# A new order of the instructions in one beat of a software-pipelined attention loop

## The chip, the core and the metric

The kernel runs on one core of a Trainium2 chip. The core's engines run in parallel, each through its own list of instructions and in that order, and they meet at semaphores: PE (TensorE, matrix products and transposes), DVE (VectorE), ACT (ScalarE), POOL (GpSimd) and SP (SyncE, here only DMA issues). The metric is the device time of one execution in microseconds, the median of several runs.

## The reference, cut to what matters

The program is a chain of four blocks: a gated linear recurrence over x of shape (8, 256, 128), six layers of windowed attention and gated feed-forward, one multi-head attention with low-rank projections, and a mixture of experts. Only the six layers are touched here. One of them, for one batch of 256 tokens:

```
qkv = shift_tokens(x) @ Wqkv            # 16 heads of 64
q, k = l2norm(q) * qs, l2norm(k) * ks
q = q*cos*scale + rotate_half(q)*sin*scale
k = k*cos/scale + rotate_half(k)*sin/scale
attn = softmax(mask(q @ k^T * 8))       # windows of 32, each sees 64 keys
x = x + (attn @ v) @ Wo
xn = layernorm(x) * g + b
a, gate = split(xn @ W1 + b1)
x = x + (a * gelu(gate)) @ W2 + b2
```

With 6 layers and 8 batches this is done 48 times. All of it is in float32.

## The kernel before

The 48 (layer, batch) pairs are the iterations i of one flow. In an iteration the attention is cut into four units (two halves of the heads times two halves of the tokens, each 128 tokens by 512 channels), and time is cut into five beats, j = 0 to 4. A unit goes through five stages, and the stages of different units overlap: in beat j the engines work on up to five units of two iterations at once.

- Stage Q (beats 0 to 3): PE multiplies q into bank 0 (L505), k into bank 1 (L507) and v into bank 2 (L539). ACT squares q (L628) and k (L642) into `sq` and copies v (L647). DVE multiplies q and k by the rotary tables, two instructions each (L723, L724). POOL adds the two products (L813, L816) and folds the squares (`sqh`, L819), and DVE sums them (L751).
- Stage T (beats 4, 0, 1, 2): POOL scales q and k by their inverse norms (L807; DVE computes these in beat 4, L701 to L706), PE turns them, q into bank 3 (L478) and k into bank 4 (L487); ACT copies them to `qT` (L661) and to `kBD` (L674, two instructions).
- Stage S (beats 0 to 3): ACT seeds bank 5 with the mask (L613), PE adds the scores (L565), DVE takes the row maximum `mx` (L746), ACT the exponentials `pr` (L666, eight instructions).
- Stage P (beats 1 to 4): PE turns `pr` into bank 6 (L516), ACT copies it to `pT` (L632), PE multiplies by v (L579), DVE sums `pr` (L731) and divides (L763).
- Stage O (beats 2, 3, 4, 0): PE turns the result into bank 4 (L529, in beat 0 L551), ACT copies it to `attT` (L637); after every second unit PE multiplies by Wo (L598).

Bank 4 is thus used twice in a beat: by the k transposes of stage T, which ACT drains with L674 (semaphore `kt_ev`), and by the transposes of stage O in the next beat, which therefore wait for that L674. Bank 1 serves the next k product once its readers are done: DVE's rotation first, ACT's square after it. `sq` is written by both squares and read by L819.

Beside the units there is the feed-forward part. Layernorm (L339 and L346 in beat 1, L353, `ln_scale` at L399 and `xnF` at L681 in beat 3), the up-projection in beat 4 (`up_pe`, L460, three chunks of which the third uses bank 6), Gelu in beat 4 (L655, with a table load before it, L623, and one after it, L657, since the exponentials need another table) and the down-projection in beat 0 (L468).

Nothing schedules at run time. The order on each engine is the order in which the functions below write it, one function for each engine, with `has(F_x)` telling whether a stage has a unit in this beat. Iterations 0 to 2 and 47 to 50 are written out, with parts missing; 3 to 46 are a loop.

Of the kernel before, what the change touches and what calls it, by code (L numbers as in the profile page):

```python
# [13 lines left out]
ALU = mybir.AluOpType  # L14
ACT = mybir.ActivationFunctionType
# [69 lines left out]
def mixed_kernel(nc, A, out):  # L85
    with ExitStack() as ctx:
# [404 lines left out]
        def layers_pe(pe):  # L491
            pe.matmul(bank[5][:, :], ident, cst("rot"), start=True, stop=True).then_inc(s_set.sem, 1)
            for i, j, live, has, unit in units(pe):
                if has(F_Q):
                    _, _, n = unit(F_Q)
                    h, t = j // NT, j % NT
                    xt = xs[:, t * P:(t + 1) * P]
                    if j == 0:
                        pe.wait_ge(xs_in.sem, xs_in.after(i))
                        if live(3):  # L500
                            pe.wait_ge(h_mul.sem, h_mul.after(i - 3))
                    if t == 0:
                        pe.wait_ge(ld_qkv[h].sem, ld_qkv[h].after(i >> 3))
                    pe.wait_ge(q_sq.sem, q_sq.after(n - 1))
                    pe.matmul(bank[0][:, :], xt, wqkv[:, h * 512:(h + 1) * 512], start=True, stop=True).then_inc(q_mm.sem, 1)  # L505
                    pe.wait_ge(k_sq.sem, k_sq.after(n - 1))
                    pe.matmul(bank[1][:, :], xt, wqkv[:, INNER + h * 512:INNER + (h + 1) * 512],  # L507
                              start=True, stop=True).then_inc(k_mm.sem, 1)
                if has(F_P):
                    _, slot, n = unit(F_P)  # L510
                    pe.wait_ge(p_exp.sem, p_exp.after(n))
                    pe.wait_ge(pt_ev.sem, pt_ev.after(n - 1))
                    if j == 1 and live(3):
                        pe.wait_ge(f_res.sem, f_res.after(i - 3))
                    for p in range(HP):
                        mm = pe.transpose(bank[6][:, p * P:(p + 1) * P],  # L516
                                          pr[:, slot % 2, 2 * p:2 * p + 2, :].rearrange("q h k -> q (h k)"), ident)
                    mm.then_inc(pt_mm.sem, 1)
                if has(F_O) and j:
                    _, slot, n = unit(F_O)  # L520
                    pe.wait_ge(o_norm.sem, o_norm.after(n))
                    pe.wait_ge(ot_ev.sem, ot_ev.after(n - 1))
                    if has(F_T):
                        _, _, nt = unit(F_T)
                        pe.wait_ge(kt_ev.sem, kt_ev.after(nt - 1))
                    else:
                        pe.wait_ge(kt_ev.sem, kt_ev.after(UPB * (i - 1) + UPB - 1) if live(1) else kt_ev.after(UPB * NI - 1))
                    for p in range(HP):
                        mm = pe.transpose(bank[4][:, p * P:(p + 1) * P],  # L529
                                          ob[:, slot % 2, 2 * p:2 * p + 2, :].rearrange("q h k -> q (h k)"), ident)  # L530
                    mm.then_inc(ot_mm.sem, 1)
                if has(F_Q):
# [8 lines left out]
                if has(F_O) and j == 0:  # L541
                    _, slot, n = unit(F_O)
                    pe.wait_ge(o_norm.sem, o_norm.after(n))
                    pe.wait_ge(ot_ev.sem, ot_ev.after(n - 1))
                    if has(F_T):
                        _, _, nt = unit(F_T)
                        pe.wait_ge(kt_ev.sem, kt_ev.after(nt - 1))
                    else:
                        pe.wait_ge(kt_ev.sem, kt_ev.after(UPB * (i - 1) + UPB - 1) if live(1) else kt_ev.after(UPB * NI - 1))
                    for p in range(HP):  # L550
                        mm = pe.transpose(bank[4][:, p * P:(p + 1) * P],  # L551
                                          ob[:, slot % 2, 2 * p:2 * p + 2, :].rearrange("q h k -> q (h k)"), ident)
                    mm.then_inc(ot_mm.sem, 1)
                if j == UPB and live(2):
                    for c in range(FC):
                        up_pe(pe, i, live, c)
                if has(F_S):
# [43 lines left out]
                if j == UPB - 1 and live(2):  # L601
                    pe.wait_ge(qt_ev.sem, qt_ev.after(UPB * (i - 1) + UPB - 1) if live(1) else qt_ev.after(UPB * NI - 1))
                    ln_turn_out(pe, i - 2, bank[3][:, 0:SEQ])
# [7 lines left out]
        def layers_act(act):  # L611
# [6 lines left out]
            for i, j, live, has, unit in units(act):  # L618
# [3 lines left out]
                if j == UPB and live(2):  # L622
                    act.preload_act_table(ACT.Gelu)  # L623
                if has(F_Q):
                    _, _, n = unit(F_Q)
                    act.wait_ge(q_mul.sem, q_mul.after(n))
                    act.wait_ge(sq_half.sem, sq_half.after(n - 1))
                    act.activation(sq[:, 0:HH, :], bank[0][:, :].rearrange("p (h d) -> p h d", d=DH), ACT.Square).then_inc(q_sq.sem, 1)  # L628
                if has(F_P):
                    _, _, n = unit(F_P)  # L630
                    act.wait_ge(pt_mm.sem, pt_mm.after(n))
                    act.activation(pT[:, :, :].rearrange("p a b -> p (a b)"), bank[6][:, :], ACT.Copy).then_inc(pt_ev.sem, 1)  # L632
# [6 lines left out]
                if has(F_Q):  # L639
                    _, _, n = unit(F_Q)  # L640
                    act.wait_ge(k_mul.sem, k_mul.after(n))
                    act.activation(sq[:, HH:, :], bank[1][:, :].rearrange("p (h d) -> p h d", d=DH), ACT.Square).then_inc(k_sq.sem, 1)  # L642
# [6 lines left out]
                if j == UPB - 1 and live(2):  # L649
                    ln_scale(act, i - 2)  # L650
# [7 lines left out]
                if has(F_T):  # L658
                    _, slot, n = unit(F_T)
                    act.wait_ge(qt_mm.sem, qt_mm.after(n))  # L660
                    act.activation(qT[:, slot % 2].rearrange("p a b -> p (a b)"), bank[3][:, :], ACT.Copy).then_inc(qt_ev.sem, 1)  # L661
# [7 lines left out]
                if has(F_T):  # L669
                    _, slot, n = unit(F_T)  # L670
                    h, t = slot // NT, slot % NT
                    act.wait_ge(kt_mm.sem, kt_mm.after(n))
# [4 lines left out]
                if j == UPB - 1 and live(2):  # L677
                    m = i - 2
                    act.wait_ge(ld_up.sem, ld_up.after(m >> 3))
                    act.wait_ge(ln_t2.sem, ln_t2.after(m))  # L680
                    act.activation(xnF[:, :], bank[3][:, 0:SEQ], ACT.Identity, bias=lngb[:, 1:2],  # L681
                                   scale=lngb[:, 0:1]).then_inc(ln_out.sem, 1)
# [25 lines left out]
        def layers_dve(dve):  # L708
            for i, j, live, has, unit in units(dve):
                if j == UPB and live(0):  # L710
                    norms(dve, i)
                if has(F_Q):
# [4 lines left out]
                    for m, (mm, mul, add) in enumerate(((q_mm, q_mul, q_add), (k_mm, k_mul, k_add))):  # L717
# [63 lines left out]
        def layers_pool(pool):  # L781
# [4 lines left out]
            for i, j, live, has, unit in units(pool):  # L786
# [22 lines left out]
                if has(F_Q):  # L809
# [8 lines left out]
                    pool.wait_ge(ss_red.sem, ss_red.after(n - 1))  # L818
                    pool.tensor_tensor(sqh[:, :, :], sq[:, :, 0:DH // 2], sq[:, :, DH // 2:], ALU.add).then_inc(sq_half.sem, 1)  # L819
# [769 lines left out]
```

## Time and profile before

| what | value |
|---|---|
| median of 3 runs | 2337.63 us (2337.19 to 2347.07) |
| profiled execution | 2337.19 us, of which the span of instructions is 2335.4 us |
| PE busy | 2159.0 us, 92% of the span |
| ACT, DVE, POOL busy | 74%, 64%, 58% |
| PE clock over the 40 slices | 1.0 or 0.9 of full from the third slice on, but for slice 34 (0.7) |
| HBM | 10 GB/s over the span |

The loop begins at about 154 us and ends at about 1794 us. In it one iteration follows another every 36.45 us, so 70% of the time is 45 equal iterations. The busy time of PE counts the tails of matrix products that overlap the next ones, so the distances between the starts of its instructions tell more than their durations. A row of the timeline gives the start, the busy time, the engine, the line, the operation, what it writes and reads, how many instructions are merged, and in brackets how long the engine sat idle before it and whose end it was waiting for.

### The profile page before, as it was taken

To read this page: it belongs to the slowest core of one execution; us is meant where nothing else is said; L and a number is where in the kernel's file an instruction comes from. 1 tells how busy PE (TensorE), PEld (TensorE's weight loads), DVE (VectorE), ACT (ScalarE), POOL (GpSimd) and SP (SyncE) were. 2 spreads that over 40 slices of the span, in tenths; PEclk is the share of its full clock that TensorE was granted. 3 is DMA by queue.
4 is the path that set the end of the run, shared out by engine and by line. 5 is a ranking of instruction groups with operands and counts; after the bars stand their busy time and mean duration, and the time that the engine had idled before them with its cause. 6 is when DMAs were issued, how large, how long until landed. Compare 5 with 4: busy or idle time off the path is not lost.

```text
span 2335.4 us, 66376 instructions
## 1 busy us (share of the span) xinstructions
PE 2159.0 (92%) x22450; PEld 1523.6 (65%) x22450; DVE 1489.0 (64%) x3344; ACT 1738.4 (74%) x4329; POOL 1365.7 (58%) x1541
## 2 busy tenths in 40 slices
PE   4799999999999999999999999999999688969999
PEld 2366666666666666666666666666666356649998
DVE  6667777677776776767767677677776366651111
ACT  2588888888888888888888888888888455534444
POOL 2787777777777777777777777777776121200000
PEclk7899999999999999999999999999999799979999
DMA  2222232222322223222232222322222200000000
GB/s 73 57 65 60 50 88 60 60 60 50 88 60 60 60 50 88 60 59 61 49 87 60 59 61 49 87 61 59 62 49 59 73 2 1 0 1 3 4 4 7
DMA packets 156775, 119.49 MB, mean 51 GB/s; under 512 B 45806, under 2 KB 148660, under 8 KB 156596
## 3 DMA queue, kind: packets, MB, share of 16 engines
q1 hardware_dynamic: 156724, 118.82, 21.3%
q8 instruction: 30, 0.49, 0.1%
q14 instruction: 21, 0.17, 0.0%
HBM read 23.28 MB, written 1.05 MB: 10 GB/s over the span
## 4 chain that ended last, share of the span: by engine, by line
PE 59%; ACT 13%; DVE 12%; issue 7%; POOL 7%; DVEq 0%; POOLq 0%; ACTq 0%
PE bank L598 7%; PE bank L565 6%; PE bank L539 5%; PE bank L1411 5%; PE bank L1402 5%; PE bank L505 4%; PE bank L579 4%; PE bank L478 4%; ACT pr L666 4%; PE bank L507 3%; POOL sqh L819 3%; POOL kr L816 3%; PE bank L468 3%; PE bank L460 2%; DVE t L724 2%
## 5 line engine op out<-in xcount | busy, mean ns | idle before, releaser
L666 ACT ACTIVATE pr<-bank,mx 128x64 f32<-128x64 f32 x1536 | 335.5, 342 | 16.6 <-DVE mx L746 16.6
L723 DVE TENSOR_TENSOR t<-bank,rot_t 128x512 f32<-128x512 f32 x384 | 262.5, 684 | 86.5 <-PE bank L505 82.5
L807 POOL TENSOR_TENSOR qr<-qr,rn 128x512 f32<-128x512 f32 x192 | 199.5, 1039 | 187.8 <-DVE rn L706 187.8
L751 DVE TENSOR_REDUCE ss<-sqh 128x16 f32<-128x512 f32 x192 | 131.7, 686 | 266.6 <-POOL sqh L819 266.6
L813 POOL TENSOR_TENSOR qr<-t 128x512 f32<-128x512 f32 x192 | 245.3, 1278 | 86.9 <-DVE t L724 86.9
L628 ACT ACTIVATE sq<-bank 128x512 f32<-128x512 f32 x192 | 114.6, 597 | 213.1 <-DVE t L724 211.8
L724 DVE TENSOR_TENSOR t<-bank,rot_t 128x512 f32<-128x512 f32 x384 | 261.5, 681 | 0.0
L816 POOL TENSOR_TENSOR kr<-t 128x512 f32<-128x512 f32 x192 | 245.1, 1277 | 0.3 <-DVE t L724 0.3
L819 POOL TENSOR_TENSOR sqh<-sq 128x512 f32<-128x512 f32 x192 | 243.8, 1270 | 0.4
L565 PEld LDWEIGHTS bank<-kBD,qT 128*32 128x32 f32 x6144 | 156.1, 109 | 116.6 <-issue 115.7
L674 ACT ACTIVATE kBD<-bank 64x512 f32<-64x512 f32 x384 | 228.7, 596 | 3.1 <-PE bank L487 0.8
L505 PE MATMUL bank<-wqkv,xs 128*128 128x512 f32 x384 | 207.2, 621 | 4.4 <-ACT sq L628 4.2
L565 PE MATMUL bank<-kBD,qT 128*32 128x128 f32 x6144 | 207.5, 276 | 0.4 <-ACT bank L613 0.3
L579 PE MATMUL bank<-vBD,pT 128*32 128x128 f32 x6144 | 206.4, 275 | 0.3 <-ACT pT L632 0.3
L807 POOL TENSOR_TENSOR kr<-kr,rn 128x512 f32<-128x512 f32 x192 | 199.7, 1040 | 0.0
L507 PE MATMUL bank<-wqkv,xs 128*128 128x512 f32 x384 | 198.0, 597 | 0.1
L1424 ACT ACTIVATE wqkv<-bank,b1e 128x256 f32<-128x256 f32 x256 | 107.0, 470 | 120.9 <-PE bank L1402 119.5
L539 PE MATMUL bank<-wqkv,xs 128*128 128x512 f32 x384 | 196.9, 595 | 0.0
L598 PE MATMUL bank<-attT,wo 128*128 128x256 f32 x768 | 186.4, 385 | 0.0
L579 PEld LDWEIGHTS bank<-vBD,pT 128*32 128x32 f32 x6144 | 159.9, 110 | 33.8 <-issue 33.3
L746 DVE TENSOR_REDUCE mx<-bank 128x8 f32<-128x512 f32 x192 | 130.5, 680 | 58.9 <-PE bank L565 58.8
L460 PE MATMUL bank<-xnF,w 128*128 128x256 f32 (+1 forms) x576 | 145.4, 389 | 19.0 <-ACT pT L632 18.2
(172 smaller groups left out, 4549.3 us busy)
## 6 DMA issues: line engine op xcount, KB each, us to landing
vBD<-vS SPq DMA_DIRECT2D x1152, 64.0 KB, 2.0
vBD<-vS SPq DMA_DIRECT2D x576, 32.0 KB, 1.9
wqkv<-in_L_ffn_Wqkv_dram SPq DMA_DIRECT2D x12, 768.0 KB, 6.4
wo<-in_L_ffn_Wo_dram SPq DMA_DIRECT2D x12, 256.0 KB, 2.8
vBD<-in_L_ffn_W_dram SPq DMA_DIRECT2D x1, 2048.0 KB, 9.3
w<-in_L_ffn_W_dram SPq DMA_DIRECT2D x6, 341.0 KB
const<-in_const_dram SPq DMA_DIRECT2D x1, 1158.0 KB, 5.2
out_dram<-acc SPq DMA_DIRECT2D x8, 128.0 KB, 1.8
```

The costliest lines, as they stand in the source:

```text
L505: pe.matmul(bank[0][:, :], xt, wqkv[:, h * 512:(h + 1) * 512], start=True, stop=True).then_inc(q_mm.sem, 1)
L507: pe.matmul(bank[1][:, :], xt, wqkv[:, INNER + h * 512:INNER + (h + 1) * 512], start=True, stop=True).then_inc(k_mm.sem, 1)
L539: pe.matmul(bank[2][:, :], xt, wqkv[:, 2 * INNER + h * 512:2 * INNER + (h + 1) * 512], start=True, stop=True).then_inc(v_mm.sem, 1)
L565: mm = pe.matmul(bank[5][w * WIN:(w + 1) * WIN, p * P:(p + 1) * P], qT[:, slot % 2, p, w * WIN:(w + 1) * WIN], kBD[:, h, p, :, k0:k0 + 2 * ...
L579: mm = pe.matmul(bank[7][w * WIN:(w + 1) * WIN, p * P:(p + 1) * P], pT[:, p, w * WIN:(w + 1) * WIN], vBD[:, h, t * NWT + w, :, p, :], star ...
L598: mm = pe.matmul(bank[2][:, 0:SEQ], wo[:, h * HP + c, :], attT[:, h * HP + c, :], start=(c == 0), stop=(c == HP - 1))
L666: ins = act.activation(pr[:, slot % 2, hd, :], bank[5][:, hd * 64:(hd + 1) * 64], ACT.Exp, bias=mx[:, slot % 2, hd:hd + 1])
L723: dve.tensor_tensor(t1[:, m], src, tab[:, 0, :].unsqueeze(1).broadcast_to([P, HH, DH]), ALU.mult)
L724: dve.tensor_tensor(t2[:, m].rearrange("p h (s d) -> p h s d", s=2), swp, tab[:, 1, :].rearrange("p (s d) -> p s d", s=2).unsqueeze(1).bro ...
L807: pool.tensor_tensor(x, x, rn[:, slot, half * HH:(half + 1) * HH].unsqueeze(2).broadcast_to([P, HH, DH]), ALU.mult).then_inc(norm.sem, 1)
L816: pool.tensor_tensor(kr[:, slot], t1[:, 1], t2[:, 1], ALU.add).then_inc(k_add.sem, 1)
L819: pool.tensor_tensor(sqh[:, :, :], sq[:, :, 0:DH // 2], sq[:, :, DH // 2:], ALU.add).then_inc(sq_half.sem, 1)
```

## The change

The arithmetic and the number of instructions stay the same. What changes is the order on PE, ACT and POOL and three semaphore waits.

- PE: in every beat the stage O transposes come before the stage P transposes (before: after them, and in beat 0 after the v product). The stage T transposes come after the stage P product (before: between scores and product). The layernorm transposes of beat 3 come before the scores. In beat 4 the third chunk of the up-projection comes after the stage P product.
- ACT: the k square comes first and the q square second, then `attT`, `pT`, `vS` (before: q square, `pT`, `attT`, k square, `vS`). The copy to `qT` comes after the exponentials instead of before. `ln_scale` comes to the head of beat 3 and `xnF` before the exponentials.
- DVE's rotation of k waits for ACT's k square (before: for the product), and bank 1 is free when DVE has rotated.
- POOL folds the squares before it adds k (before: after).

The diff, without the blocks that only move:

```diff
             if c == 1:
-                pe.wait_ge(k_sq.sem, k_sq.after(UPB * i + UPB - 1) if live(0) else k_sq.after(UPB * NI - 1))
+                pe.wait_ge(k_mul.sem, k_mul.after(UPB * i + UPB - 1) if live(0) else k_mul.after(UPB * NI - 1))
...
-                    pe.wait_ge(k_sq.sem, k_sq.after(n - 1))
+                    pe.wait_ge(k_mul.sem, k_mul.after(n - 1))
                     pe.matmul(bank[1][:, :], xt, wqkv[:, INNER + h * 512:INNER + (h + 1) * 512],
                               start=True, stop=True).then_inc(k_mm.sem, 1)
-                if has(F_P):
...
-                    mm.then_inc(pt_mm.sem, 1)
-                if has(F_O) and j:
+                if has(F_O):
                     _, slot, n = unit(F_O)
                     pe.wait_ge(o_norm.sem, o_norm.after(n))
...
                     mm.then_inc(ot_mm.sem, 1)
+                if has(F_P):
...
+                    mm.then_inc(pt_mm.sem, 1)
...
-                if has(F_O) and j == 0:
...
-                    mm.then_inc(ot_mm.sem, 1)
                 if j == UPB and live(2):
-                    for c in range(FC):
+                    for c in range(2):
                         up_pe(pe, i, live, c)
+                if j == UPB - 1 and live(2):
...
+                    ln_turn_out(pe, i - 2, bank[3][:, 0:SEQ])
                 if has(F_S):
...
-                if has(F_T) and j < UPB:
-                    turn_qk(pe, i, j, live, has, unit)
                 if has(F_P):
...
+                if j == UPB and live(2):
+                    up_pe(pe, i, live, 2)
+                if has(F_T) and j < UPB:
+                    turn_qk(pe, i, j, live, has, unit)
...
+                if j == UPB - 1 and live(2):
+                    ln_scale(act, i - 2)
                 if has(F_Q):
                     _, _, n = unit(F_Q)
+                    act.wait_ge(k_mm.sem, k_mm.after(n))
+                    act.wait_ge(sq_half.sem, sq_half.after(n - 1))
+                    act.activation(sq[:, HH:, :], bank[1]..., ACT.Square).then_inc(k_sq.sem, 1)
                     act.wait_ge(q_mul.sem, q_mul.after(n))
-                    act.wait_ge(sq_half.sem, sq_half.after(n - 1))
                     act.activation(sq[:, 0:HH, :], bank[0]..., ACT.Square).then_inc(q_sq.sem, 1)
...
-                if has(F_T):
-                    act.wait_ge(qt_mm.sem, qt_mm.after(n))
-                    act.activation(qT[:, slot % 2]..., bank[3][:, :], ACT.Copy).then_inc(qt_ev.sem, 1)
                 if has(F_S):
...
                 if has(F_T):
+                    act.wait_ge(qt_mm.sem, qt_mm.after(n))
+                    act.activation(qT[:, slot % 2]..., bank[3][:, :], ACT.Copy).then_inc(qt_ev.sem, 1)
                     act.wait_ge(kt_mm.sem, kt_mm.after(n))
...
-                    for m, (mm, mul, add) in enumerate(((q_mm, q_mul, q_add), (k_mm, k_mul, k_add))):
+                    for m, (mm, mul, add) in enumerate(((q_mm, q_mul, q_add), (k_sq, k_mul, k_add))):
...
+                    pool.wait_ge(q_sq.sem, q_sq.after(n))
+                    pool.wait_ge(ss_red.sem, ss_red.after(n - 1))
+                    pool.tensor_tensor(sqh[:, :, :], sq[:, :, 0:DH // 2], sq[:, :, DH // 2:], ALU.add).then_inc(sq_half.sem, 1)
                     pool.wait_ge(k_mul.sem, k_mul.after(n))
                     pool.wait_ge(kt_mm.sem, kt_mm.after(n - UPB))
                     pool.tensor_tensor(kr[:, slot], t1[:, 1], t2[:, 1], ALU.add).then_inc(k_add.sem, 1)
-                    pool.wait_ge(k_sq.sem, k_sq.after(n))
...
```

PE in beat 2, before. The line numbers are those of each program: `ob` is stage O's transpose, `pr` stage P's, `kBD,qT` the scores, `vBD,pT` the product with v.

```order
L505 MATMUL bank<-wqkv,xs 128x512
L507 MATMUL bank<-wqkv,xs 128x512
L516 MATMUL bank<-const,pr 128x128 x4
L529 MATMUL bank<-const,ob 128x128 x4
L539 MATMUL bank<-wqkv,xs 128x512
L565 MATMUL bank<-kBD,qT 32x128 x16
L478 MATMUL bank<-const,qr 128x128 x4
L487 MATMUL bank<-const,kr 128x128 x4
L579 MATMUL bank<-vBD,pT 32x128 x16
```

PE in beat 2, now:

```order
L505 MATMUL bank<-wqkv,xs 128x512
L507 MATMUL bank<-wqkv,xs 128x512
L519 MATMUL bank<-const,ob 128x128 x4
L529 MATMUL bank<-const,pr 128x128 x4
L539 MATMUL bank<-wqkv,xs 128x512
L555 MATMUL bank<-kBD,qT 32x128 x16
L567 MATMUL bank<-vBD,pT 32x128 x16
L478 MATMUL bank<-const,qr 128x128 x4
L487 MATMUL bank<-const,kr 128x128 x4
```

The `ob` transposes, which wait for the `kBD` copies of the beat before, moved ahead of the `pr` transposes, and the 32-column products now stand next to each other.

ACT in beat 2, before (`sq` first of q, then of k):

```order
L613 ACTIVATE bank<-const 128x512
L628 ACTIVATE sq<-bank 128x512
L632 ACTIVATE pT<-bank 128x512
L637 ACTIVATE attT<-bank 128x4x128
L642 ACTIVATE sq<-bank 128x512
L645 REGISTER_ALU
L647 ACTIVATE vS<-bank 128x4x2x64
L660 REGISTER_ALU
L661 ACTIVATE qT<-bank 128x512
L666 ACTIVATE pr<-bank,mx 128x64 x8
L674 ACTIVATE kBD<-bank 64x4x128 x2
```

ACT in beat 2, now (L619 squares k, L621 q):

```order
L602 ACTIVATE bank<-const 128x512
L619 ACTIVATE sq<-bank 128x512
L621 ACTIVATE sq<-bank 128x512
L626 ACTIVATE attT<-bank 128x4x128
L631 ACTIVATE pT<-bank 128x512
L636 ACTIVATE vS<-bank 128x4x2x64
L655 ACTIVATE pr<-bank,mx 128x64 x8
L661 REGISTER_ALU
L662 ACTIVATE qT<-bank 128x512
L665 ACTIVATE kBD<-bank 64x4x128 x2
```

The k square moved from fourth to first among the copies, and `qT` moved from before the exponentials to between them and `kBD`.

PE at the head of beat 0, before:

```order
L505 MATMUL bank<-wqkv,xs 128x512
L507 MATMUL bank<-wqkv,xs 128x512
L539 MATMUL bank<-wqkv,xs 128x512
L551 MATMUL bank<-const,ob 128x128 x4
L565 MATMUL bank<-kBD,qT 32x128 x16
```

The same place now:

```order
L505 MATMUL bank<-wqkv,xs 128x512
L507 MATMUL bank<-wqkv,xs 128x512
L519 MATMUL bank<-const,ob 128x128 x4
L539 MATMUL bank<-wqkv,xs 128x512
L555 MATMUL bank<-kBD,qT 32x128 x16
```

Here the `ob` transposes moved ahead of the v product.

## Rows read from the trace of the kernel before

**Rows 1.** Waits of PE, 400 to 1600 us: total us, times, longest

```profile
PE bank L529 <- DVE ob L763: 16.5, 33, 0.5
PE bank L460 <- ACT pT L632: 12.8, 33, 0.4
PE bank L529 <- ACT kBD L674: 12.4, 32, 0.4
```

**Rows 2.** Busy us by stretch: length, PE, PEld, DVE, ACT, POOL, PE clock, DMA share, GB/s

```profile
115.00:119.00 4.00, 1.44 (x17) 1.00 (x10) 2.59 (x8) 0.60 (x1) 2.68 (x3) 1.00 0.40 93
...
1000.00:1036.45 36.45, 35.17 (x384) 23.95 (x383) 26.18 (x57) 31.02 (x78) 27.21 (x30) 1.00 0.30 68
```

**Rows 3.** Timeline of all engines, beat 1 of one iteration

```profile
1000.32 1.02 PE L505 MATMUL bank<-wqkv,xs 128*128 128x512 f32 x2
...
1001.18 1.02 PE L507 MATMUL bank<-wqkv,xs 128*128 128x512 f32 x2
...
1001.38 0.69 DVE L723 TENSOR_TENSOR t<-bank,rot_t 128x512 f32<-128x512 f32 x1 [0.25 <-PE bank L505]
...
1002.70 0.60 ACT L628 ACTIVATE sq<-bank 128x512 f32<-128x512 f32 x1 [1.89 <-DVE t L724]
...
1003.19 0.59 ACT L632 ACTIVATE pT<-bank 128x512 f32<-128x512 f32 x1
...
1003.43 1.08 PE L565 MATMUL bank<-kBD,qT 128*32 128x128 f32 x32
...
1004.44 0.66 PE L478 MATMUL bank<-const,qr 128*128 128x128 f32 x4
...
1004.61 0.67 DVE L746 TENSOR_REDUCE mx<-bank 128x8 f32<-128x512 f32 x1
...
1005.62 1.74 ACT L666 ACTIVATE pr<-bank,mx 128x64 f32<-128x64 f32 x8
...
1007.19 1.21 ACT L674 ACTIVATE kBD<-bank 64x512 f32<-64x512 f32 x2
```

**Rows 4.** The same timeline, beats 2 and 3

```profile
1011.75 0.68 DVE L731 TENSOR_REDUCE psm<-pr 128x8 f32<-128x512 f32 x1
...
1013.36 0.66 DVE L746 TENSOR_REDUCE mx<-bank 128x8 f32<-128x512 f32 x1
...
1014.06 1.12 PE L505 MATMUL bank<-wqkv,xs 128*128 128x512 f32 x2
...
1015.64 1.21 ACT L674 ACTIVATE kBD<-bank 64x512 f32<-64x512 f32 x2
...
1016.90 0.66 PE L529 MATMUL bank<-const,ob 128*128 128x128 f32 x4 [0.39 <-ACT kBD L674]
...
1018.35 1.08 PE L565 MATMUL bank<-kBD,qT 128*32 128x128 f32 x32
...
1019.25 1.06 PE L579 MATMUL bank<-vBD,pT 128*32 128x128 f32 x32
```

**Rows 5.** The same timeline, beat 4, beat 0 and the next beat 1

```profile
1022.35 0.66 PE L516 MATMUL bank<-const,pr 128*128 128x128 f32 x4
...
1023.01 0.59 ACT L613 ACTIVATE bank<-const 128x512 f32<-128x512 f32 x1
...
1025.56 1.09 PE L460 MATMUL bank<-xnF,w 128*85 128x256 f32 x4 [0.39 <-ACT pT L632]
...
1027.18 1.28 ACT L657 ACT_TABLE_LOAD   x1
...
1028.59 1.12 PE L505 MATMUL bank<-wqkv,xs 128*128 128x512 f32 x2
...
1028.97 1.18 ACT L674 ACTIVATE kBD<-bank 64x512 f32<-64x512 f32 x2
...
1031.27 0.60 PE L551 MATMUL bank<-const,ob 128*128 128x128 f32 x4
...
1036.77 1.02 PE L505 MATMUL bank<-wqkv,xs 128*128 128x512 f32 x2
```

More of the change, by code:

```diff
@@ L531, in layers_pe @@
                     mm.then_inc(ot_mm.sem, 1)
+                if has(F_P):
+                    _, slot, n = unit(F_P)
+                    pe.wait_ge(p_exp.sem, p_exp.after(n))
+                    pe.wait_ge(pt_ev.sem, pt_ev.after(n - 1))
+                    if j == 1 and live(3):
+                        pe.wait_ge(f_res.sem, f_res.after(i - 3))
+                    for p in range(HP):
+                        mm = pe.transpose(bank[6][:, p * P:(p + 1) * P],
+                                          pr[:, slot % 2, 2 * p:2 * p + 2, :].rearrange("q h k -> q (h k)"), ident)
+                    mm.then_inc(pt_mm.sem, 1)
                 if has(F_Q):
@@ L540, in layers_pe @@
                               start=True, stop=True).then_inc(v_mm.sem, 1)
-                if has(F_O) and j == 0:
-                    _, slot, n = unit(F_O)
-                    pe.wait_ge(o_norm.sem, o_norm.after(n))
-                    pe.wait_ge(ot_ev.sem, ot_ev.after(n - 1))
-                    if has(F_T):
[L546 to L552, printed above, removed]
-                    mm.then_inc(ot_mm.sem, 1)
                 if j == UPB and live(2):
-                    for c in range(FC):
+                    for c in range(2):
                         up_pe(pe, i, live, c)
+                if j == UPB - 1 and live(2):
+                    pe.wait_ge(qt_ev.sem, qt_ev.after(UPB * (i - 1) + UPB - 1) if live(1) else qt_ev.after(UPB * NI - 1))
+                    ln_turn_out(pe, i - 2, bank[3][:, 0:SEQ])
                 if has(F_S):
@@ L600, in layers_pe @@
                     mm.then_inc(y_mm.sem, 1)
-                if j == UPB - 1 and live(2):
-                    pe.wait_ge(qt_ev.sem, qt_ev.after(UPB * (i - 1) + UPB - 1) if live(1) else qt_ev.after(UPB * NI - 1))
-                    ln_turn_out(pe, i - 2, bank[3][:, 0:SEQ])
                 if j == 1 and live(2):
@@ L623, in layers_act @@
                     act.preload_act_table(ACT.Gelu)
+                if j == UPB - 1 and live(2):
+                    ln_scale(act, i - 2)
                 if has(F_Q):
                     _, _, n = unit(F_Q)
+                    act.wait_ge(k_mm.sem, k_mm.after(n))
+                    act.wait_ge(sq_half.sem, sq_half.after(n - 1))
+                    act.activation(sq[:, HH:, :], bank[1][:, :].rearrange("p (h d) -> p h d", d=DH), ACT.Square).then_inc(k_sq.sem, 1)
                     act.wait_ge(q_mul.sem, q_mul.after(n))
-                    act.wait_ge(sq_half.sem, sq_half.after(n - 1))
                     act.activation(sq[:, 0:HH, :], bank[0][:, :].rearrange("p (h d) -> p h d", d=DH), ACT.Square).then_inc(q_sq.sem, 1)
[L629 to L632, printed above, removed]
                 if has(F_O):
@@ L638, in layers_act @@
                                    bank[4][:, :].rearrange("p (a b) -> p a b", a=HP), ACT.Copy).then_inc(ot_ev.sem, 1)
[L639 to L642, printed above, removed]
+                if has(F_P):
+                    _, _, n = unit(F_P)
+                    act.wait_ge(pt_mm.sem, pt_mm.after(n))
+                    act.activation(pT[:, :, :].rearrange("p a b -> p (a b)"), bank[6][:, :], ACT.Copy).then_inc(pt_ev.sem, 1)
                 if has(F_Q):
@@ L649, in layers_act @@
                 if j == UPB - 1 and live(2):
-                    ln_scale(act, i - 2)
+                    m = i - 2
+                    act.wait_ge(ld_up.sem, ld_up.after(m >> 3))
+                    act.wait_ge(ln_t2.sem, ln_t2.after(m))
+                    act.activation(xnF[:, :], bank[3][:, 0:SEQ], ACT.Identity, bias=lngb[:, 1:2],
+                                   scale=lngb[:, 0:1]).then_inc(ln_out.sem, 1)
                 if j == UPB and live(2):
@@ L671, in layers_act @@
                     h, t = slot // NT, slot % NT
+                    act.wait_ge(qt_mm.sem, qt_mm.after(n))
+                    act.activation(qT[:, slot % 2].rearrange("p a b -> p (a b)"), bank[3][:, :], ACT.Copy).then_inc(qt_ev.sem, 1)
                     act.wait_ge(kt_mm.sem, kt_mm.after(n))
@@ L676, in layers_act @@
                     ins.then_inc(kt_ev.sem, 1)
[L677 to L682, printed above, removed]
                 if j == 1 and live(2):
```

13 lines of the change are left out of this document (removed).

## The prediction, made before the changed kernel ran

> **What bounds the kernel now.** I read the busy shares first, then PE's waits, then the timeline of one iteration. Of one iteration of 36.45 us PE is busy 35.17 us, ACT 31.02, POOL 27.21 and DVE 26.18, at full clock [rows 2]. PE's starts follow each other with almost no holes. Its waits in 1200 us (33 iterations) are three, each once an iteration: for DVE's division 16.5 us, for the `pT` copy in beat 4 12.8 us, for `kBD` in beat 3 12.4 us [rows 1]. That is 41.7 / 33 = 1.26 us an iteration. So PE bounds the loop, nothing can give back much more than these 1.26 us, and a new wait on PE is paid in full, since PE runs in order. The question is what each change does to the moment at which PE's head instruction may start.
>
> The Trainium skill ("Perfetto Trace Analysis", Identifying the Most-Contended Engine) says that matmul busy time judges headroom badly and that the weight-load share is the better measure. That share is 23.95 of 36.45 us, 66% [rows 2]; by the rule a third of PE would be free, and waits of some us would change nothing (2337 us). The spacing of starts speaks against it here. The argument below does not use either.
>
> **What the change takes away.** Times from here on are us after 1000 in the trace. From the scores to the transposes behind them PE needs 1.01 us (3.43 to 4.44) [rows 3], from the scores straight to the product with v 0.90 (18.35 to 19.25) [rows 4]. In beats 1 and 2 these products now stand together, and there are two changes from one kind of product to the other instead of four. One change is worth these 0.11 us or a little more; two of them are 0.22 to 0.3, and I take 0.27 us off each of the two beats. The folding on POOL comes 1.27 us earlier, which lets DVE divide earlier; this removes the 0.5 us wait of beat 2.
>
> **What it adds: a walk through one iteration.** Rules, all from rows: an instruction starts 0.04 us after what it waits for ends; a full ACT copy takes 0.60, the next starts 0.49 after its start (2.70, 3.19); a DVE instruction takes 0.68, the next starts 0.60 after; a product can be read 1.06 after its start (0.32 to 1.38); the k product starts 0.86 after the q product (1.18) [rows 3].
>
> *Beat 1*, from PE's q product at 0.32. The k square starts at 1.18 + 1.06 = 2.24 and ends at 2.84. DVE has issued both q instructions by 2.58 but must now wait for the square, until 2.88: 0.30 later than before. So `mx` moves from 4.61 to 4.91 and ends at 5.58. The exponentials start at 5.62, as before, because `qT` no longer stands in front. Their eight issues take 1.57 (5.62 to 7.19), then comes `qT` with 0.49, and `kBD` starts at 7.68 and ends at 8.87, where it ended at 8.40 [rows 3]. PE meanwhile starts beat 2 at 6.49: before, the distance from there to beat 1's q product was 6.43 (the wait for the division and the stage O transposes take beat 2 from 6.43 to 7.31, up to 14.06 [rows 4]), now it is 6.17.
>
> *Beat 2.* PE issues q and k (6.49, 7.35) and could issue the `ob` transposes at 8.21. They wait for `kBD`: 8.91. Before, they waited up to 0.5 longer, for the division [rows 1], but `pr` had been turned by then; now `pr` is behind them. So the gain is small. ACT goes on with the layernorm copy and the seed, and the k square starts at 9.79. I take 0.92 from the end of `kBD` for these: 0.59 for the seed [rows 5] and 0.33 for the copy of 256 columns, which lies between the issue of a 64-column exponential, 0.20, and that of a 512-column copy, 0.49. DVE finished q at about 9.4 and now stands until 10.43. From there: k 1.20, `psm` at 11.63, `mx` 1.61 behind it (11.75 to 13.36) [rows 4], so 13.24 to 13.91. Exponentials 13.95, `qT` 15.52, `kBD` 16.01 to 17.20. Before it started at 15.64 and ended at 16.85 [rows 4]: 0.35 later, though PE is 0.2 us ahead. The product with v waits for `pT` (two squares and `attT` stand in front of it: 9.79 + 3 x 0.49 + 0.60 = 11.86) and costs 0.1. PE ends its beat at 13.84 instead of 14.06.
>
> *Beat 3.* q and k at 13.84 and 14.70, the `ob` transposes could go at 15.56 and go at 17.24. This is the main cost: 1.7 us of nothing, where the kernel before turned `pr` and waited 0.39 [rows 4]. Before, beat 4 began 5.45 after them (22.35 - 16.90) [rows 4, 5]. Now `pr` stands in this stretch too, +0.44; the layernorm's transposes between v and the scores cost nothing more; and the product with v waits for `pT`, about 0.3, since `ln_scale` and both squares are ahead of it on ACT (17.20 + 0.5 seed + 0.8 `ln_scale`, then 4 x 0.49 + 0.1: 20.53). Less 0.04 of spacing, beat 4 begins at 23.39 instead of 22.35.
>
> *Beat 4.* In beat 3 the k square ends at 19.08, so DVE has `mx` 0.04 + 2 x 0.60 + 0.83 later at 21.15 to 21.82, and the exponentials hold ACT from 21.86 for 1.57; the seed starts at 23.43 instead of 23.01 [rows 5]. `attT` now stands before `pT`, so `pT`, which ended just before the third chunk's 25.56, ends at 25.51 + 0.42 + 0.49 = 26.42. PE has two chunks of the up-projection ahead of it and starts the product with v at 26.46, the third chunk 1.01 later at 27.47; before, that chunk started at 25.56. The last Gelu hangs on it: the second table load was at 27.18, that is 1.62 after the chunk, and will be at 29.09. `kBD` started 1.79 behind the load (28.97) and ends at 30.15 [rows 5]; it will end at 32.06. PE itself, with chunk and transposes behind the product with v, is done 2.1 us after the chunk's start, at 29.6 (before 28.59, the transposes and the product with v being the 3.03 from 25.56) [rows 5].
>
> *Beat 0.* PE issues q and k at 29.6 and 30.46 and could turn `ob` at 31.3, but bank 4 is free at 32.10: 0.8 us. Before, these transposes came behind v and did not wait (31.27) [rows 5]. The rest, from the transposes to beat 1, was 5.50 (31.27 to 36.77) [rows 5] with v in front; with v behind, 0.84 more: 38.44.
>
> The period is then 38.44 - 0.32 = 38.12 instead of 36.45: +1.67 us. By beats 1, 2, 3, 4, 0: -0.26, +0.04, +1.26, -0.03, +0.66. In beat 1 ACT stands where it stood against PE (`kBD` ends as the q product starts), so the next iteration repeats this one.
>
> **The other parts.** The edits of bank 1's wait (`k_mul` in place of `k_sq`) cost nothing: the rotation is done 2.9 us before the next k product. `ln_scale` at the head of beat 3, two instructions of 128 columns, takes between 2 x 0.20 and 2 x 0.49 of ACT, I take 0.8 (nearer to the longer row), ahead of the k square and delays `mx`; the path there goes on to Wo, which is not waiting, and 0.42 of it is the seed's shift above. Were there no cover for it, up to 0.8 us an iteration would come on top. POOL's k addition now comes 1.27 later; its reader is four beats away, in beat 4 the norms, which follow Wo. SP's moves and loads are issued behind the same semaphores and have whole beats of slack. Bounds of the sum: each new wait may be absent (-1.7 to beat 3, -0.8 to beat 0), which with all the savings gives a period of 34.6; or the loop through ACT and DVE may be longer by its own rounding, some 0.05 at each of ten handovers, +0.5 us.
>
> **Sum.** Iterations 3 to 47 have all stages: 45 x 1.67 = 75 us. In iterations 1 and 2 beat 3's wait exists without the feed-forward part: about 1 us each. That makes 77 us on the profiled execution's 2337.19, 2414; the median of the runs, 2337.63, is the same within 0.5.
>
> **Rivals.**
> 1. *Faster.* The `kBD` copies come in time after all. That needs ACT to end them by 15.6 in beat 3, 1.6 us sooner than I walk, for instance if the k square did not hold DVE. For it: ACT is busy only 31.02 of 36.45 [rows 2]. Against: its idle time lies before the squares, where it waits for DVE, 1.89 us in beat 1 [rows 3], and cannot be moved behind the exponentials. All waits gone and 0.54 saved: -1.8 x 45 = -81, 2256 us. In part, 2300.
> 2. *Only one of the two new waits* holds, beat 3's. Then +1.67 - 0.8 = 0.87 x 45, 2377 us. This is so if the third chunk's Gelu reaches ACT 0.8 us sooner.
> 3. *No change*: gains and waits balance, 2337 us. It needs beat 3's `kBD` at the old distance from PE. Above I find it 0.35 later and needed 1.3 us earlier.
> 4. *The clock falls* in the new wait of 1.7 us. In the fill of the pipeline PE was busy 1.44 of 4.00 us and the granted clock stayed 1.00, the level of 2.4 GHz [rows 2], so I do not expect it. If 6 us of PE work an iteration ran at 1.2 GHz, it would be +270 us, some 2680. The Trainium skill ("TensorE: Matmul & The Clock Gate", HAM oscillation) warns that recurring idle gaps of PE can drop the clock; these rows do not show it for gaps of this size.
>
> **How the numbers follow.** Forecast 0.75, one wait only 0.08, clock 0.02, no change 0.05, faster 0.10. Within 0.5% (11.7 us, about what can be told from nothing) 0.05, slower 0.85, faster 0.10. The forecast's own range is 2385 to 2440: +0.5 us of period gives 2437, and a beat 0 wait of nearly nothing some 2385. To leave out no more than 2 in 10 I reach down into the case of one wait and halfway to no change: 2355 to 2440.
>
> **What would show it.** Right: a period near 38.1; the `ob` transposes waiting for `kBD` in beats 2, 3 and 0, about 0.7, 1.7 and 0.8 us; DVE waiting for the k square in beat 2 by about 1 us; the wait for DVE's division gone; score and v products 0.90 apart; clock 1.00. Wrong: a period under 37, or `kBD` ending earlier against PE's q product than 15.64 + 1.21 - 14.06 = 2.8 us in beat 3; a wait of PE on something I have not named would refute the walk even if the total came out.

## The result, and the profile after

The changed kernel takes 2434.22 us (median of 4 runs, 2433.63 to 2439.07). The kernel before, with a fourth run, has a median of 2342.20 (2337.19 to 2347.07); the ratio is 1.0397, with a 95% interval of 1.0365 to 1.0431. The profiled execution took 2438.54 us, with a span of 2436.7 us. The forecast was 2414, the range 2355 to 2440.

The timeline of the changed kernel, one iteration, the instructions of the walk. L505 and L507 are the q and k products, L519 turns `ob`, L665 is `kBD`, L619 the k square, L655 the exponentials, L567 the product with v.

```profile
1000.92 1.12 PE L505 MATMUL bank<-wqkv,xs 128*128 128x512 f32 x2 [0.26 <-DVE hT L723]
...
1003.17 0.66 PE L519 MATMUL bank<-const,ob 128*128 128x128 f32 x4 [0.28 <-ACT kBD L665]
...
1009.59 1.02 PE L505 MATMUL bank<-wqkv,xs 128*128 128x512 f32 x2
...
1015.73 1.02 PE L505 MATMUL bank<-wqkv,xs 128*128 128x512 f32 x2
...
1018.21 0.66 PE L519 MATMUL bank<-const,ob 128*128 128x128 f32 x4 [0.59 <-ACT kBD L665]
...
1019.60 0.69 DVE L708 TENSOR_TENSOR t<-bank,rot_t 128x512 f32<-128x512 f32 x1 [0.91 <-ACT sq L619]
...
1023.12 1.74 ACT L655 ACTIVATE pr<-bank,mx 128x64 f32<-128x64 f32 x8 [1.60 <-DVE mx L731]
1023.22 1.02 PE L505 MATMUL bank<-wqkv,xs 128*128 128x512 f32 x2
...
1024.71 0.65 ACT L662 ACTIVATE qT<-bank 128x512 f32<-128x512 f32 x1
...
1025.18 1.21 ACT L665 ACTIVATE kBD<-bank 64x512 f32<-64x512 f32 x2
...
1026.45 0.66 PE L519 MATMUL bank<-const,ob 128*128 128x128 f32 x4 [1.35 <-ACT kBD L665]
...
1028.44 0.69 DVE L708 TENSOR_TENSOR t<-bank,rot_t 128x512 f32<-128x512 f32 x1 [2.88 <-ACT sq L619]
...
1029.93 1.08 PE L567 MATMUL bank<-vBD,pT 128*32 128x128 f32 x32 [0.30 <-ACT pT L631]
...
1032.77 0.60 PE L519 MATMUL bank<-const,ob 128*128 128x128 f32 x4
...
1036.01 1.08 PE L567 MATMUL bank<-vBD,pT 128*32 128x128 f32 x32 [0.47 <-ACT pT L631]
1037.02 1.09 PE L460 MATMUL bank<-xnF,w 128*85 128x256 f32 x4
...
1038.64 1.28 ACT L650 ACT_TABLE_LOAD   x1
...
1039.41 1.12 PE L505 MATMUL bank<-wqkv,xs 128*128 128x512 f32 x2 [0.25 <-DVE hT L723]
...
1040.43 1.18 ACT L665 ACTIVATE kBD<-bank 64x512 f32<-64x512 f32 x2
```

The q product of beat 0 stands at 0.92 and again at 39.41: 38.49 us an iteration instead of 36.45. The waits of PE, which in [rows 1] were three of at most 0.5 us:

```profile
PE bank L519 <- ACT kBD L665: 69.1, 94, 1.4
PE bank L567 <- ACT pT L631: 24.0, 62, 0.5
PE bank L505 <- DVE hT L723: 8.0, 31, 0.3
```

The wait for DVE's division is gone. DVE and ACT now wait for each other:

```profile
DVE t L708 <- ACT sq L619: 134.2, 125, 2.9
```

```profile
ACT pr L655 <- DVE mx L731: 135.4, 124, 1.6
```

Before, ACT waited for DVE too, but in front of the q square, and DVE had no wait for ACT worth listing:

```profile
ACT sq L628 <- DVE t L724: 143.3, 99, 1.9
ACT pr L666 <- DVE mx L746: 11.4, 33, 0.3
```

So what is new is the closed loop: the exponentials and `kBD` on ACT, then the k square on ACT, then DVE's rotation and maximum, then the exponentials again. The chain that ended last runs over these two engines from the k square at 11.51 (beat 1) to the `pT` copy at 35.47 (beat 4), without a piece of PE. Its part in beats 3 and 4:

```profile
1025.80 0.59 ACT kBD L665
1026.39 0.49 ACT bank L602
1026.91 0.69 ACT lnx L399 x2
1027.81 0.61 ACT sq L619
1028.44 0.69 DVE t L708
...
1030.48 0.68 DVE mx L731
1031.18 1.75 ACT pr L655 x8
...
1036.01 1.08 PE bank L567 x32
```

Most of the loss arises here. From `kBD` of beat 2 to `kBD` of beat 4 the kernel before took 13.33 us (15.64 to 28.97 in [rows 4] and [rows 5]); now it takes 15.25 (25.18 to 40.43), 1.92 more. `ln_scale` (L399), now at the head of beat 3, is one of the links: 0.90 us from its start to that of the k square.

And the busy time of that iteration, to be laid beside [rows 2]: the engines do the same work, at full clock, in a longer time.

```profile
1000.92:1039.41 38.49, 35.14 (x383) 23.89 (x383) 26.29 (x58) 31.07 (x78) 27.15 (x31) 1.00 0.25 58
```

### The profile page after: what moved, and what is told of

Read it like the earlier page. It is cut to its first block, busy times and chain, and to the rows that moved or that the text cites. A ratio compares the mean times of both kernels' runs of the same rounds, so it can differ in the third digit from the quotient of the medians.

```text
span 2436.7 us, 66368 instructions
## 1 busy us (share of the span) xinstructions
PE 2160.2 (89%) x22442; PEld 1526.2 (63%) x22450; DVE 1494.2 (61%) x3344; ACT 1741.2 (71%) x4329; POOL 1363.5 (56%) x1541
## 4 chain that ended last, share of the span: by engine, by line
PE 36%; ACT 34%; DVE 18%; issue 8%; POOL 1%; ACTq 0%; another core or an unknown queue 0%; DVEq 0%; POOLq 0%
ACT pr L655 10%; ACT kBD L665 7%; PE bank L1396 5%; PE bank L1387 5%; DVE t L708 4%; DVE mx L731 4%; DVE psm L716 3%; DVE t L709 3%; ACT sq L619 3%; PE bank L590 3%; ACT bank L602 3%; PE bank L468 3%; PE bank L460 2%; PE bank L555 2%; PE bank L567 2%
## 5 line engine op out<-in xcount | busy, mean ns | idle before, releaser
L655 ACT ACTIVATE pr<-bank,mx 128x64 f32<-128x64 f32 x1536 | 335.0, 329 | 210.0 <-DVE mx L731 210.0
L567 PE MATMUL bank<-vBD,pT 128*32 128x128 f32 x6144 | 206.5, 275 | 41.3 <-ACT pT L631 36.8
L665 ACT ACTIVATE kBD<-bank 64x512 f32<-64x512 f32 x384 | 228.8, 596 | 3.1 <-PE bank L487 0.8
L519 PEld LDWEIGHTS bank<-const,ob 128*128 128x128 f32 x768 | 84.5, 141 | 233.3 <-ACT kBD L665 206.4
L519 PE MATMUL bank<-const,ob 128*128 128x128 f32 x768 | 123.2, 283 | 112.1 <-ACT kBD L665 110.5
L505 PE MATMUL bank<-wqkv,xs 128*128 128x512 f32 x384 | 201.8, 607 | 15.5 <-DVE hT L723 11.5
L567 PEld LDWEIGHTS bank<-vBD,pT 128*32 128x32 f32 x6144 | 161.7, 110 | 83.8 <-ACT pT L631 68.5
L539 PE MATMUL bank<-wqkv,xs 128*128 128x512 f32 x384 | 196.5, 593 | 0.0
L507 PE MATMUL bank<-wqkv,xs 128*128 128x512 f32 x384 | 196.1, 592 | 0.0
L619 ACT ACTIVATE sq<-bank 128x512 f32<-128x512 f32 x192 | 114.3, 595 | 66.3 <-PE bank L507 64.0
```

Of the source, the lines that this page charges most:

```text
L519: mm = pe.transpose(bank[4][:, p * P:(p + 1) * P], ob[:, slot % 2, 2 * p:2 * p + 2, :].rearrange("q h k -> q (h k)"), ident)
L567: mm = pe.matmul(bank[7][w * WIN:(w + 1) * WIN, p * P:(p + 1) * P], pT[:, p, w * WIN:(w + 1) * WIN], vBD[:, h, t * NWT + w, :, p, :], star ...
L655: ins = act.activation(pr[:, slot % 2, hd, :], bank[5][:, hd * 64:(hd + 1) * 64], ACT.Exp, bias=mx[:, slot % 2, hd:hd + 1])
L665: ins = act.activation(kBD[64 * e:64 * e + 64, h, :, e, WIN + t * P:WIN + (t + 1) * P], bank[4][64 * e:64 * e + 64, :].rearrange("p (a b) ...
```

## The experiments

The theories. Theory 1 is the prediction's: each wait of PE in front of the `ob` transposes is paid because of the place that they have on PE. Theory 2 came out of the chain shown above: from beat 1 to beat 4 a loop ACT - DVE - ACT sets the pace, and PE waits beside it. Theory 3, on the place of the `qT` copy, was formed after the second experiment. The period column is read from the timeline of each run.

| kernel | median us | ratio to before (95%) | us an iteration |
|---|---|---|---|
| before | 2338 to 2342 | 1 | 36.45 |
| changed | 2434.22 | 1.0397 (1.0365 to 1.0431) | 38.49 |
| a1 | 2410.82 | 1.0305 (1.0284 to 1.0327) | 37.98 |
| a2 | 2450.05 | 1.0472 (1.0450 to 1.0493) | 38.76 |
| a3 | 2369.95 | 1.0134 (1.0110 to 1.0157) | 37.02 |
| a4 | 2406.83 | 1.0293 (1.0268 to 1.0317) | 37.87 |
| c1 | 2335.65 | 0.9989 (0.9980 to 0.9999) | 36.45 |
| b1 | 2352.83 | 1.0069 (1.0048 to 1.0091) | 36.56 |
| b2 | 2283.13 | 0.9765 (0.9749 to 0.9782) | 35.29 |
| d1 | 2363.08 | 1.0102 (1.0085 to 1.0118) | 36.98 |
| g1 | 2308.23 | 0.9865 (0.9830 to 0.9901) | 35.77 |
| d2 | 2307.70 | 0.9864 (0.9828 to 0.9900) | 35.76 |
| e1 | 2315.98 | 0.9891 (0.9859 to 0.9924) | 35.98 |
| h1 | 2292.55 | 0.9795 (0.9762 to 0.9827) | 35.35 |

**a1, a2, a3, a4: one part undone in the changed kernel.**

```diff
 a1, PE's order
-O transposes; P transposes; v product          # all beats
+P transposes; O transposes; v product          # beats 2 to 4
+v product; O transposes                        # beat 0
```

> The changed kernel (2434 us) with one part undone: on PE the stage P transposes stand before those of stage O again, and in beat 0 the v product does too. Theory 1, PE's order: PE stands still in front of the ob transposes for 0.6, 1.4 and 0.3 us in beats 2, 3 and 0 while work behind them is ready; with the order back, 0.44 us of that work fills each of the waits of beats 2 and 3 and about 0.4 us that of beat 0: 45 x 1.3 = -58 us, 2376. Theory 2, a loop through ACT and DVE: from beat 1 to beat 4 the end is set by ACT's kBD, seed, k square, DVE's rotation, maximum and ACT's exponentials, and PE only waits beside it, so filling PE's waits of beats 2 and 3 gives nothing; only beat 0, where the chain does run over PE, gives 0.4 us: 45 x 0.4 = -19 us, 2415, with PE's waits in beats 2 and 3 moved, not gone.

2411: theory 2, within 4 us. The part costs 0.51 us an iteration. PE's waits have moved to the product with v, behind `pT` (41.5 us, where they were 24.0), and DVE and ACT still wait 136.9 and 124.8 us for each other.

```profile
PE bank L580 <- ACT pT L644: 41.5, 96, 0.6
PE bank L529 <- ACT kBD L678: 32.7, 63, 0.9
PE bank L505 <- DVE hT L736: 8.1, 32, 0.3
```

So filling a wait of PE is worth little where PE is not what the loop runs over.

```diff
 a2, ACT
+                if has(F_T):
+                    act.activation(qT..., bank[3], ACT.Copy)    # before the exponentials
                 if has(F_S):
                     ... ACT.Exp ...
-                    act.activation(qT..., bank[3], ACT.Copy)
```

> The changed kernel with one part undone: ACT copies qT before the exponentials again. Theory 2 (the loop through ACT and DVE): the copy goes into time in which ACT waits for mx (135 us in 124 waits), and kBD ends 0.49 us earlier in beats 1 and 2, both on the loop: 45 x 0.98 = -44 us, 2390. Theory 1 (only PE's order at the ob transposes): the same 0.49 at each of the two waits, but the wait of beat 2 does not carry over into beat 3's, so at most 0.5 an iteration, -22 us, 2412.

2450, slower: both theories missed. The copy does not find idle time, it makes a wait. The change turns q after the product with v, and in front of the exponentials ACT then stands for PE, up to 1.7 us, 93 times:

```profile
ACT qT L654 <- PE bank L478: 126.5, 93, 1.7
```

The later copy in the change is the answer to the later transposes. This is theory 3.

```diff
 a3, ACT, DVE, PE, POOL
-ACT: k square (k_mm); q square (q_mul); ...
+ACT: q square (q_mul); attT; pT; k square (k_mul); ...
-DVE: rotate k after k_sq       PE: k product after k_mul    POOL: fold after q_sq
+DVE: rotate k after k_mm       PE: k product after k_sq     POOL: fold after k_sq
```

> The changed kernel with one part undone: ACT squares q first and k fourth again, DVE's rotation of k waits for the product only, bank 1 for the k square, and POOL's fold (still before the k addition) for the k square. Theory 2: DVE no longer waits for ACT (134 us of waits in 1200 us go), the loop is cut in beats 1 to 3, kBD comes about 0.8 us earlier in beat 2 and mx about 1.3 us in beat 3; PE's chain takes over in beat 4: 45 x 1.15 = -52 us, 2382. Theory 1: the wait in front of ob in beat 3 shrinks by 0.8, -36 us, 2398. If neither holds and the order of the squares is harmless: no change.

2370, 64 us less: the largest single cost, 1.47 us an iteration, and beyond theory 2's 52. `kBD` of beat 2 now starts 1.57 us after beat 3's q product (24.92 to 26.49) instead of 1.96 (23.22 to 25.18), and DVE's wait for the k square is gone.

```profile
1024.92 1.02 PE L505 MATMUL bank<-wqkv,xs 128*128 128x512 f32 x2
...
1026.49 1.21 ACT L667 ACTIVATE kBD<-bank 64x512 f32<-64x512 f32 x2
```

```diff
 a4, PE in beat 4
-up c=0, c=1; product with v; up c=2
+up c=0, c=1, c=2; product with v
```

> The changed kernel with one part undone: the third chunk of the up-projection stands before the stage P product again. Both theories: the last Gelu, the second table load and kBD of beat 4 come 1.0 us earlier, the wait for bank 4 in beat 0 (0.43) and that of the q product for hT (0.25) go: 45 x 0.65 = -29 us, 2405. If the chunk costs only by the q product's wait for hT: -11 us, 2423.

2407 for 2405: both theories gave this number, so the run does not tell them apart. The table load hangs on the last chunk, as in the walk. The wait for `hT` is gone, and the `ob` transposes of beat 0 no longer wait (64 waits for `kBD` instead of 94).

**c1: all of a1, a3 and a4 undone together.**

> The changed kernel with four parts undone: PE's ob transposes behind pr and behind v, q squared first and DVE's rotation of k not waiting for ACT, the third chunk before the product. Left of the change are the products side by side, qT behind the exponentials, attT before pT, the earlier fold and the moved layernorm. If the costs found singly (24, 64 and 27 us) add up: 2434 - 115 = 2319. By a walk through beats 1 to 3 with the earlier division (mx in beat 2 at 12.1 instead of 13.4): 35.5 us an iteration, 2296. If the kBD wait of beat 3 stays as it was before: 2338.

2336, the level of before, and the last of the three values on record. The costs overlap: 24 + 64 + 27 = 115 us less would be 2319, and 99 came back; PE's wait for `kBD` is 20.7 us, more than the 12.4 of before. What is left of the change, with the earlier fold in it, was expected to win and does not. The next runs say why.

**b1, b2, d1: parts alone in the kernel before.**

```diff
 b1, PE (d1: also the qT copy behind the exponentials on ACT)
-                if has(F_T) and j < UPB:
-                    turn_qk(...)
                 if has(F_P):
                     ... product with v ...
+                if has(F_T) and j < UPB:
+                    turn_qk(...)
```

> The kernel before with one part of the change alone: on PE the stage T transposes come behind the stage P product. Reading of the run before this (theory 3): the q transposes then come 0.9 us later in beats 1 and 2, ACT, which copies qT before the exponentials here, waits for them, and exponentials and kBD come about 0.5 us later each time; the spacing gained does not help: 36.45 becomes about 36.9 us, 2358. Theory of the prediction (the product costs nothing but saves 0.27 in two beats): -24 us, 2314.

> The kernel before with two parts of the change: the stage T transposes behind the stage P product, and qT copied behind the exponentials. Theory 3 (the copy's place has to match the transposes' place): the exponentials are no longer held, but kBD still ends 0.47 us later, and beat 3 waits for it: about 36.8 us, 2355, the same as with the first part alone or slightly less. If it is the exponentials alone that matter: 36.2 us, 2326.

2353 and 2363, both slower. In b1 ACT waits for PE's q transposes, 1.5 us an iteration, but only 0.1 of it reaches the period. In d1, with the later copy, `kBD` comes later and the wait of beat 3 grows from 12.4 to 28.7 us in 1200.

```profile
ACT qT L661 <- PE bank L478: 49.1, 65, 1.0
```

```profile
PE bank L529 <- ACT kBD L672: 28.7, 33, 0.9
```

Theory 3's sizes were off by 5 and 8 us. It had both runs slower than before, which held, but d1 no slower than b1, which did not: the later copy costs another 0.4 us an iteration. The saving in spacing was never seen as time. b1's median lies between two pairs of runs, 2347 and 2349, and 2357 and 2359; its period of 36.56 makes 5 us, so its cost is known only as some 5 to 15 us.

```diff
 b2, POOL
-q addition; k addition; fold (k_sq)
+q addition; fold (k_sq); k addition
```

> The kernel before with one part of the change alone: POOL folds the squares before it adds k. Theory of the prediction: DVE divides up to 1.27 us earlier, PE's wait of 0.5 us in beat 2 goes: -22 us, 2316. If beat 2 is held by the kBD of beat 3 anyway, part of it comes back there and it is -10 us, 2328.

2283, 55 us faster: two and a half times the larger of the two values that I had on record for this part (22 and 10). Two of the three waits of [rows 1] are gone:

```profile
PE bank L460 <- ACT pT L632: 12.8, 34, 0.4
```

The iteration of 35.29 us holds 34.91 us of PE work:

```profile
1006.95:1042.24 35.29, 34.91 (x383) 24.07 (x382) 26.37 (x57) 31.14 (x79) 27.21 (x30) 1.00 0.25 56
```

The earlier fold lets DVE divide earlier. In beat 2 the division starts 2.01 us after the q product before, and 0.80 us after it in b2. First the kernel before:

```profile
1006.75 1.02 PE L505 MATMUL bank<-wqkv,xs 128*128 128x512 f32 x2
...
1008.76 0.68 DVE L763 TENSOR_TENSOR ob<-bank,rinv 128x512 f32<-128x512 f32 x1
```

Then b2:

```profile
1013.38 1.02 PE L505 MATMUL bank<-wqkv,xs 128*128 128x512 f32 x2
...
1014.18 0.68 DVE L763 TENSOR_TENSOR ob<-bank,rinv 128x512 f32<-128x512 f32 x1
```

Everything behind the division on DVE is earlier too: `mx` of beat 2 starts 5.40 us after the q product instead of 6.61, and `kBD` ends 2.30 us after beat 3's q product instead of 2.79, so PE no longer waits for it. Beat 2 is 0.72 us shorter (6.59) and beat 3 0.48 (7.81).

**g1, d2, e1: the earlier fold plus one other part, in the kernel before.**

```diff
 g1: b2, and a3's edit the other way (k square first, DVE's rotation waits)
 d2: b2, and d1's
 e1: b2, and in beat 3
+PE: layernorm transposes before the scores
+ACT: ln_scale before the q square; xnF before the exponentials
```

> The kernel before with two parts of the change: POOL's earlier fold (2283 us alone) and the k square first on ACT with DVE's rotation of k waiting for it. Theory 2 (a loop ACT - DVE - ACT): the coupling costs here too, without any of the moves on PE: kBD 0.3 us later in beat 1, 0.9 in beat 2, mx still later in beat 3; about +1.4 us an iteration on 35.29: 2346. If the coupling is only harmful together with the moved transposes: within 10 us of 2283.

> The kernel before with three parts of the change: the earlier fold (2283 alone), the stage T transposes behind the stage P product, and qT behind the exponentials. Theory 3 (kBD ends a qT copy later and beat 3 waits for it, whatever is saved in spacing): 35.29 + 0.45 us, 2304. If the spacing gained (0.27 in two beats) is free now that the waits are gone: 2259.

> The kernel before with the earlier fold (2283 alone) and the three layernorm moves of beat 3 (the transposes before the scores, ln_scale at the head, xnF before the exponentials). By a walk: the exponentials of beat 3 end 0.2 us earlier against PE, since xnF no longer stands behind them, so the seed and pT of beat 4 too: 2274. If ln_scale at the head holds q's square and with it the fold and pT: up to +0.8 us an iteration, 2319.

2308, 2308 and 2316: each costs 25, 25 and 33 us on 2283. For g1 theory 2 had the sign and not the size (63). In beat 2, where PE's q product starts at 25.00, the k square starts at 27.48, so DVE waits 0.44 and not 0.9; in beat 3 DVE waits 1.51, but PE has Wo to do before it needs what is late.

```profile
1025.00 1.02 PE L505 MATMUL bank<-wqkv,xs 128*128 128x512 f32 x2
...
1027.48 0.59 ACT L628 ACTIVATE sq<-bank 128x512 f32<-128x512 f32 x1
...
1028.11 0.69 DVE L721 TENSOR_TENSOR t<-bank,rot_t 128x512 f32<-128x512 f32 x1 [0.44 <-ACT sq L628]
...
1034.47 0.66 PE L529 MATMUL bank<-const,ob 128*128 128x128 f32 x4 [0.39 <-ACT kBD L672]
1034.93 0.60 ACT L628 ACTIVATE sq<-bank 128x512 f32<-128x512 f32 x1
...
1035.56 0.69 DVE L721 TENSOR_TENSOR t<-bank,rot_t 128x512 f32<-128x512 f32 x1 [1.51 <-ACT sq L628]
```

The same edit costs 25 us here and 64 in the change. That PE's order there makes the delayed `kBD` and `mx` count is my reading; no run takes these two parts alone. d2 met theory 3 within 4 us. e1 took the second reading, the held copies: Wo waits for `vS` and the exponentials end later, so beat 4's `pr` transposes wait for them.

```profile
1008.55 1.99 PE L601 MATMUL bank<-attT,wo 128*128 128x256 f32 x8 [0.24 <-ACT vS L649]
...
1010.62 0.42 PEld L516 LDWEIGHTS bank<-const,pr 128*128 128x128 f32 x4 [0.48 <-ACT pr L672]
```

d2 and e1 together (25 + 33 = 58) put the kernel that has both at 2341; c1, which has both and `attT` before `pT`, measured 2336. In periods the sum is exact: 35.29 + 0.47 + 0.69 = 36.45, which is c1's. So this is where c1's expected gain went. `attT` before `pT` was not run alone; by this sum it costs nothing. Nor were the layernorm moves undone in the changed kernel, where `ln_scale` stands in the chain shown above; what they cost there stays open.

**h1: an attempt at the last wait.**

```diff
-act.preload_act_table(ACT.Gelu)     # head of beat 4
 pT; attT
+act.preload_act_table(ACT.Gelu)
```

> Not a part of the change: the kernel before with the earlier fold (2283 alone), and in beat 4 the Gelu table load behind the pT and attT copies instead of before them. The only wait of PE left, 0.4 us an iteration for pT in beat 4, should go, and the Gelus start where they did, because the load only changes places with the copies: 45 x 0.39 = -18 us, 2265. If the copies need more than the idle time that the load used: no change.

No gain (35.35 us an iteration). The wait for `pT` went, and PE waits behind POOL's scaling of k, which follows DVE's norms, and in front of the q product instead. The timed median is 9 us above b2's while the profiled periods agree within 0.06. On record the difference goes along with the granted clock: the one run of h1 at a mean of 0.975 took 2281.95, the other four, at 0.970 to 0.972, took 2291.80 to 2295.74, and b2's four ran at 0.974 to 0.976. What lowered the clock in those runs the record does not show.

```profile
PE bank L487 <- POOL kr L806: 6.8, 34, 0.2
PE bank L505 <- issue: 5.8, 30, 0.2
```

## Why the prediction was right

- *PE bounds the kernel before, and at most 1.26 us an iteration can be won.* It held: the best kernel, b2, wins 1.16, with PE at 34.91 of 35.29.
- *Beats 1 and 2.* Predicted 6.17 and 7.35, measured 6.14 (9.59 to 15.73) and 7.49. The `ob` transposes of beat 2 wait for `kBD`: 0.59 is shown, and from 17.45, where they could start, it is 0.76, for 0.7 predicted. DVE waits 0.91 for the k square in beat 2, for about 1. The 0.27 of spacing appeared in beat 1 (0.29).
- *Beat 3.* Predicted 9.55, measured 9.55 (23.22 to 32.77). The wait is shown as 1.35; from where L519 could start, at 24.94, to 26.45 it is 1.51, for 1.68 in the walk. What follows the wait takes 6.32 and not 6.15. The two misses cancel, so that the beat fits to 0.01 is luck.
- *Beat 4.* Predicted 6.21, measured 6.64: the term that was too small. The walk let the seed follow the exponentials by issue (0.04 into the beat); it waits for their end (32.96, 0.19). And it left out that the next q product waits for the last `hT`, which hangs on the late third chunk: 0.25. The prediction had said that a wait of PE which it did not name would refute the walk even if the total came out. This is such a wait, 31 times in the 1200 us; by that sign the walk is refuted at the end of beat 4, while the waits that it named are all there.
- *Beat 0.* Predicted 8.84, measured 8.67. PE comes later, so the wait for bank 4 is 0.4 and not 0.8; 0.10 more between the q and k products and 0.08 more behind the wait make up part of it.
- *Sum.* +2.04 an iteration and not +1.67; 45 x 2.04 = 92, and the medians differ by 92 to 97 (2434.2 against 2338 to 2342). The range's upper end, 2440, came from 0.5 us of rounding at ten handovers. The missing 0.37 came instead from beat 4 (+0.43) and beat 2 (+0.14), less 0.20 in the others; that the range held it is in part luck.
- *A bound.* The prediction's lower bound of the period was added up wrongly: without the two new waits the period is 38.12 - 1.7 - 0.8 = 35.6. Its 34.6 is the kernel before without its own waits and with the spacing won (36.45 - 1.26 - 0.54).
- *The clock.* It stayed at 1.00 with waits of 1.4 us.
- *The words.* That a new wait of PE is paid in full, since PE runs in order, was too simple. In a1 work of PE filled these waits again, 1.3 us of it by theory 1, and only 0.51 came back, since beats 2 and 3 run over ACT and DVE. The walk had that loop in it; the words did not.
- *The weight-load share.* It was 66% in [rows 2] and is 68% (24.07 of 35.29) in the fastest kernel, in which PE's starts leave no hole but one of 0.4 us. The rule of the Trainium skill ("Perfetto Trace Analysis", Identifying the Most-Contended Engine) would see a third of PE free; for this mix of transposes, 32-column products and float32 products the distance between starts was the measure that held.
- *The fold.* Priced at beat 2's 0.5 us. Alone it is worth 1.16: 0.72 in beat 2, and 0.48 in beat 3, because the time won on DVE also reaches `kBD`. In the change this gain is inside the total; the other parts cost 2434 - 2283 = 151 us.

## What to carry to other kernels

In a software-pipelined loop each edit of an order has to be walked through the other engines' orders up to the next buffer that is reused: here the `ob` transposes, the third chunk and the k square, each moved a few places, cost 24, 27 and 64 us in 2434, and the one part that helps (POOL's fold, 55 us) was buried in a bundle. Test the parts of such a change alone, in both directions; the earlier fold alone is the kernel to keep, at 2283.13 us. And a new wait of one engine for a neighbour that in turn waits for it closes a loop. Here the length of that loop, and not the busiest engine, then set the pace from beat 1 to beat 4.

## What the runs showed that I had not expected

- An edit can be good or bad by another's place: `qT` behind the exponentials saves 16 us in the change (2434 against 2450) and costs 10 in the kernel before (2363 against 2353; by the periods 0.4 us an iteration, 19 us).
- Putting the two 32-column products side by side goes with 35.14 us of PE work an iteration for 35.17 in the busy count, and with 0.29 less in beat 1's starts (6.14 for 6.43), but in no kernel here did it shorten the iteration.
